# Sixteen-head attention sequence: GpSimd's work after making an input is put in another order

## The chip, the cores and the metric

One core of one Trainium2 chip runs the whole kernel in a single launch. The metric is the device time of one execution in microseconds (us), lower is better. The engines are TensorE (PE in the profile), VectorE (DVE), ScalarE (ACT), GpSimd (POOL) and the DMA queue of SyncE (SP). Each runs its own instructions in order and waits for the others through semaphores.

## The reference, cut to what matters

Two transformer-like layers over `x` of 32 entries x 128 tokens x 128 channels in float32, with a context of 32 x 120 x 128. Four stages: cross attention with 8 heads, a feed-forward network in which the 512 best of 1536 channels are chosen per entry group (`top_k`), cross attention with 16 heads over the context, and a last stage with latent self attention of 16 heads and a mixture of experts.

```python
x = x + _L0_xattn_ref(ctx_1024, _layernorm(x), mask, ...)
x = x + _L0_ffn_ref(_layernorm(x), Wm, Wp, Wc1, Wc2)   # top_k(ck, 512) after each of its steps
x = x + _L1_xattn_ref(_layernorm(x), ctx_1024, ctx_1024, mask, w_q, w_k, w_v, w_o)
x = x + _L1_ffn_ref(_layernorm(x), g1, Wq, Wdkv, Wuk, Wuv, Wo, g2, gate_w, w1, w2)
# _L1_ffn_ref: x = x + _mla(_rmsnorm(x, g1)); x = x + _moe(_rmsnorm(x, g2))
```

The change touches the two 16-head attentions alone, which one function (`attentions16`) runs as one sequence of 64 inputs.

## The kernel before

`mega_kernel` runs the stages one after the other: 8-head attention, feed-forward, the 16-head sequence, mixture of experts. In the 16-head sequence inputs 0 to 31 are the entries of the cross attention (120 keys, names with `l1`) and inputs 32 to 63 the same entries for the latent attention (128 keys, names with `mla`). `run_pair_steps` calls `body(n)` for n = -2 to 65 on each engine; even and odd steps are unrolled in some stretches and run in hardware loops (`Fori`) of two steps in the others. Nothing but the order of each `body` and the semaphores sets the order of the work: there is no planner.

What step n does, engine by engine, in the order of its queue:

- **TensorE**: turns (transposes) probability group 3 of input n-1, turns the normalised input n+1 (`turn_input`, L1482, waits for GpSimd's `z_made`), projects the output of n-2 (L1547), turns group 2 of n-1, projects q, k and v of n+1 (L1493 to L1495), multiplies groups 0 and 1 of n-1 with the values (L1536, L1539), turns group 1 of n, multiplies groups 2 and 3 of n-1, in even steps totals the search's counts (L1552), computes the scores of n+1 (L1509 bias, L1514, waits for `q_spread` and `k_copied`), turns group 0 of n.
- **VectorE**: copies the turned input n+1 out of PSUM (`copy_input`, L1453 or L1455), copies group 3 of n-1 (L1462), adds a projection (L1678), takes the second maximum (L1644), statistics (L1684), shifts scores (L1654), copies group 1 of n, copies the values of n+1 (L1470), inverts the sums (L1663), in even steps reads a digit of the search (`read_digit`, L1697), scales the output (L1669), and takes the first maximum of input n+1 (`max_a`, L1636). At the end of step 16 it has `second_half` of the search (L1703 to L1709 and the helper at L1261), at the end of steps 17 and 34 `mla_moments`.
- **ScalarE**: copies q (L1579), copies group 2 of n-1 (L1462), copies k (L1586), in even steps the third trial of a search round (`try_number`, L1610), the second exponential (`exp_b`, L1602), in odd steps the first two trials of the next round, copies group 0 of n (L1462), and the eight first exponentials of input n+1 (`exp_a`, L1594), which wait for `max_a`.
- **GpSimd**: makes the input n+1 (`centre` L1746, `norm_output` L1760 for the second layer only, `norm_input` L1754, which writes `zn`), spreads the queries of n+1 into `QX` (`spread_q`, L1767, waits for `q_copied`), then in even steps updates the search (`next_trials(k - 1)` with k = n // 2, four tiny operations L1777 to L1783, the first of which waits for the digit that VectorE reads in this step), and in some steps computes a power, that is inverse roots of variances (L125): `later_scales` in steps -2 to 1 and `mla_scales` in steps 18, 19, 34, 35, 36 and 37. The power of step 18 waits for the moments that VectorE takes at the end of step 17, the one of step 34 for those that it takes at the end of step 34.
- **SyncE** loads the contexts two inputs ahead.

The search finds the 512th largest of 1536 logits, two bits a round; its 16 rounds are spread over the first 34 steps, two steps each. A round is: three counts on ScalarE (two in an odd step, one in the even step after it), a total on TensorE, a digit on VectorE, an update of bounds on GpSimd. After eight rounds `second_half` makes the keys of the lower half.

Of the kernel before, what the change touches and what calls it, by code (L numbers as in the profile page):

```python
# [15 lines left out]
B = 32  # L16
# [1221 lines left out]
ROUNDS = 8  # L1238
# [28 lines left out]
CHANGE = 12  # L1267


def run_pair_steps(eng, body):  # L1270

    for n in range(-2, 4):
        body(n, n % 2, n // 2)
    with eng.Fori(0, ROUNDS - 2) as i:
        body(2 * i + 4, 0, i + 2, True)
        body(2 * i + 5, 1, i + 2, True)
    for n in range(2 * ROUNDS, 2 * ROUNDS + 4):
        body(n, n % 2, n // 2)  # L1280
    with eng.Fori(0, B // 2 - 3 - ROUNDS) as i:
        body(2 * i + 2 * ROUNDS + 4, 0, i + ROUNDS + 2, True)
        body(2 * i + 2 * ROUNDS + 5, 1, i + ROUNDS + 2, True)
    for n in range(B - 2, B + 6):
        body(n, n % 2, n // 2)
    with eng.Fori(0, B // 2 - 4) as i:
        body(2 * i + B + 6, 0, None, False)
        body(2 * i + B + 7, 1, None, False)
    for n in range(PAIR - 2, PAIR + 2):
        body(n, n % 2, None)  # L1290


def attentions16(nc, phase, psum, X2, X3, stats6, mean, rstd, mhalf, small, ident, ident_bf, cols,
# [8 lines left out]
    with ExitStack() as sems, ExitStack() as st:  # L1302
# [170 lines left out]
        with nc.Block() as block:  # L1473
# [157 lines left out]
            def _(dve):  # L1631
# [16 lines left out]
                def shift_b(n, par, l1):  # L1648
                    if there(n):
                        K = keys(n, l1)  # L1650
                        wait(dve, max_b_taken, n + 1)
                        wait(dve, turned[3], n - 1)
                        wait(dve, turned[2], n - 1)
                        dve.tensor_tensor(probs[par][:, 8:16, 0:K].rearrange("p (c j) k -> p c j k", c=2),  # L1654
                                          psum[:, 2:4, 0:4 * K].rearrange("p c (j k) -> p c j k", k=K),
                                          n_max[par][:, 8:16].rearrange("p (c j) -> p c j", c=2).unsqueeze(3).broadcast_to([P, 2, 4, K]),
                                          ALU.add).then_inc(b_shifted, 1)
# [54 lines left out]
                def body(n, par, k, l1=None):  # L1712
                    copy_input(dve, n + 1, l1)
                    copy_group(dve.tensor_copy, dve, n - 1, 3, l1)
                    add_projection(n - 2, l1)
                    max_b(n, par, l1)
                    take_stats(n - 2, l1)
                    shift_b(n, par, l1)
                    copy_group(dve.tensor_copy, dve, n, 1, l1)
                    copy_values(dve.tensor_copy, dve, n + 1, 1 - par, l1)  # L1720
                    if router and par == 0 and k is not None and round_there(k - 1):
                        wait(dve, totalled, k)
                    invert_sums(n - 1)
                    if router and par == 0 and k is not None:
                        read_digit(k - 1)
                    scale_out(n - 1)
                    max_a(n + 1, 1 - par, l1)
                    if router and par == 0 and isinstance(k, int) and k == ROUNDS:
                        second_half()
                    if isinstance(n, int) and n == 2 * ROUNDS + 1:  # L1730
                        mla_moments(slice(0, CHANGE), 6)
                    if isinstance(n, int) and n == B + 2:
                        mla_moments(slice(CHANGE, B), 12)
# [4 lines left out]
            @block.gpsimd  # L1738
            def _(pool):
                def centre(m, l1):  # L1740
                    if there(m):
                        l1 = is_l1(m, l1)
                        wait(pool, z_made, m)
                        if not l1:
                            wait(pool, x_out_made, m - B)
                        pool.tensor_tensor(centred[:, :], row(X2, m, l1), of_entry(mean if l1 else mla_mean, m, l1).broadcast_to([P, D]),  # L1746
                                           ALU.subtract).then_inc(x_centred, 1)

                def norm_input(m, l1):
                    if there(m):  # L1750
                        l1 = is_l1(m, l1)
                        wait(pool, x_centred, m + 1)
                        wait(pool, z_turned, m)
                        pool.tensor_tensor(zn[:, :], centred[:, :], of_entry(rstd if l1 else mla_scale, m, l1).broadcast_to([P, D]),  # L1754
                                           ALU.mult).then_inc(z_made, 1)

                def norm_output(m, l1):
                    if there(m) and not is_l1(m, l1):
                        wait(pool, x_centred, m + 1)
                        pool.tensor_tensor(row(X3, m, False), centred[:, :], of_entry(mla_rstd, m, False).broadcast_to([P, D]),  # L1760
                                           ALU.mult).then_inc(x_out_made, 1)

                def spread_q(m, par):
                    if there(m):
                        wait(pool, q_copied, m + 1)
                        wait(pool, scored, m - 1)
                        pool.tensor_tensor(QX[par][:, :, :], qT[:, :].unsqueeze(1).broadcast_to([P, 4, P]),  # L1767
                                           own_slots[:, :].unsqueeze(2).broadcast_to([P, 4, P]), ALU.mult).then_inc(q_spread, 1)

                def next_trials(k):  # L1770
                    if round_there(k):
                        t = search
                        wait(pool, digit_read, k + 1)
                        wait(pool, trials_ready, k)
                        if isinstance(k, int) and k == ROUNDS:
                            wait(pool, halved, 4)
                        pool.tensor_tensor(t["below"][:, :], t["below4"][:, :], t["digit4"][:, :], ALU.subtract).then_inc(below_made, 1)  # L1777
                        wait(pool, below_made, k + 1)
                        pool.tensor_tensor(t["bias"][:, :], t["offsets"][:, :], t["below"][:, :].broadcast_to([P, 3]), ALU.add).then_inc(bias_made, 1)
                        wait(pool, bias_made, k + 1)  # L1780
                        pool.tensor_tensor(t["below4"][:, :], t["below"][:, :], t["four"][:, :], ALU.mult).then_inc(below4_made, 1)
                        wait(pool, below4_made, k + 1)
                        pool.tensor_tensor(t["per_unit"][:, :], t["per_unit"][:, :], t["four"][:, :], ALU.mult).then_inc(trials_ready, 1)  # L1783

                def later_scales(n):
                    if isinstance(n, int) and n < 2:
                        inverse_roots(pool, rstd, small[:, 0, :], mhalf, slice(FIRST + 7 * (n + 2), FIRST + 7 * (n + 3))).then_inc(scales_made, 1)
                    if isinstance(n, int) and n == 2:
                        pool.wait_ge(scales_made, 4)

                def mla_scales(n):
                    half = CHANGE + (B - CHANGE) // 2
                    for at, some, ready in ((2 * ROUNDS + 2, slice(0, CHANGE), 3), (B + 2, slice(CHANGE, half), 5), (B + 4, slice(half, B), 5)):
                        if isinstance(n, int) and n == at:
                            pool.wait_ge(var_ready, ready)
                            inverse_roots(pool, mla_rstd, small[:, 0, :], mhalf, some).then_inc(mla_scales_made, 1)
                        if isinstance(n, int) and n == at + 1:
                            inverse_roots(pool, mla_scale, small[:, 1, :], mhalf, some).then_inc(mla_scales_made, 1)
                    if isinstance(n, int) and n in (B - 2, PAIR - 2):
                        pool.wait_ge(mla_scales_made, 2 if n < B else 6)  # L1800

                def body(n, par, k, l1=None):
                    centre(n + 1, l1)
                    norm_output(n + 1, l1)
                    norm_input(n + 1, l1)
                    spread_q(n + 1, 1 - par)
                    if router and par == 0 and k is not None:
                        next_trials(k - 1)
                    later_scales(n)
                    mla_scales(n)  # L1810

                run_pair_steps(pool, body)

            @block.sync
# [394 lines left out]
```

## Time and profile before

| | us |
|---|---|
| median of 3 runs | 1333.4 (1332.63 to 1336.6) |
| the profiled execution | 1335.86 |
| its span in the trace | 1333.7 |
| TensorE busy | 1230.1 (92%) |
| VectorE busy | 927.5 (70%) |
| ScalarE busy | 798.9 (60%) |
| GpSimd busy | 588.9 (44%) |

The 16-head sequence takes from about 598 to 1073 us of the span. A profile row gives an instruction (line of kernel.py, engine, operation), its start and duration, and in square brackets how long its engine sat idle before it and what released it. The times of a step are read here from one `max_a` (L1636) to the next, since each step has one.

### The profile page before, as it was taken

Reading aid. Unit: us, or ns where it says so; the run is one execution under the profiler, and the core shown is the slowest. Engines: PE = TensorE matmul, PEld = TensorE weight load, DVE = VectorE, ACT = ScalarE, POOL = GpSimd, SP = SyncE. Lnnn points to the kernel's source line nnn. Section 1 sums busy time; section 2 is a strip of 40 time slices with the busy share of each in tenths; the row PEclk is TensorE's granted clock in tenths of the full one; section 3 lists DMA queues with packets and bytes.
Section 4 is the critical chain, followed back from the end, with each engine's and each line's share of the span. In section 5 each row is a group of like instructions: output and inputs, shape, how many; then the busy total and the mean of one; then the engine's idle time right before and its main releaser. Section 6 shows DMA issues by size and latency. Waiting matters only on the chain. (4 is left out here: it accounts for less than half of the span.)

```text
span 1333.7 us, 37978 instructions
## 1 busy us (share of the span) xinstructions
PE 1230.1 (92%) x13719; PEld 879.3 (66%) x13719; DVE 927.5 (70%) x2003; ACT 798.9 (60%) x2101; POOL 588.9 (44%) x673
## 2 busy tenths in 40 slices
PE   1899999999999995978999899989999979999996
PEld 0466666666666663436777777768888847777775
DVE  6476676677677673766999889979999955343431
ACT  0578878878878862325777677756666633333332
POOL 3577566666656655104223332343333223333343
PEclk9899999999999997987999899989999979999998
DMA  8000000000000000000000002000000000000000
GB/s 216 13 1 1 0 0 0 0 0 0 0 0 0 0 1 1 0 4 10 11 9 8 10 10 69 3 2 1 0 0 0 0 1 9 9 8 8 8 11 16
DMA packets 22740, 14.71 MB, mean 11 GB/s; under 512 B 6378, under 2 KB 21610, under 8 KB 22540
## 3 DMA queue, kind: packets, MB, share of 16 engines
q1 hardware_dynamic: 22520, 13.75, 3.8%
q8 instruction: 43, 0.70, 0.2%
q14 instruction: 29, 0.24, 0.1%
q10 hardware_dynamic: 148, 0.01, 0.0%
HBM read 11.66 MB, written 2.10 MB: 10 GB/s over the span
## 5 line engine op out<-in xcount | busy, mean ns | idle before, releaser
L690 POOL TENSOR_TENSOR r_norm<-ssm,mhalf 128x24 f32<-128x24 f32 x32 | 134.9, 4215 | 162.7 <-DVE ssm L595 162.7
L1767 POOL TENSOR_TENSOR pair_QX<-pair_qT,own_slots 128x512 f32<-128x512 f32 x64 | 66.7, 1041 | 257.7 <-ACT pair_qT L1579 257.7
L1985 ACT ACTIVATE moe_hid<-psum 128x512 f32<-128x512 f32 x128 | 76.4, 598 | 137.5 <-PE psum L1919 137.5
L1525 PE MATMUL psum<-ident,pair_probs 128*120 128x128 f32 (+1 forms) x1024 | 154.6, 285 | 0.7 <-ACT pair_probs L1594 0.6
L533 ACT ACTIVATE l_probs<-psum,l_n_max 128x248 f32<-128x248 f32 x256 | 117.2, 481 | 57.7 <-DVE l_n_max L613 57.7
L2143 POOL TENSOR_TENSOR moe_acc<-moe_acc,moe_prod 128x512 f32<-128x512 f32 x64 | 81.3, 1271 | 147.4 <-DVE moe_prod L2099 147.4
L1594 ACT ACTIVATE pair_probs<-psum,pair_n_max 128x120 f32<-128x120 f32 (+1 forms) x512 | 137.7, 380 | 10.4 <-DVE pair_n_max L1636 5.0
L1929 PEld LDWEIGHTS psum<-w,moe_hid 128*128 128x128 f32 x1024 | 123.1, 192 | 26.8 <-issue 26.8
L2099 DVE TENSOR_TENSOR moe_prod<-psum,moe_combine 128x512 f32<-128x512 f32 x64 | 44.3, 692 | 135.8 <-PE psum L1929 135.7
L1525 PEld LDWEIGHTS psum<-ident,pair_probs 128*120 128x120 f32 (+1 forms) x1024 | 111.3, 141 | 28.6 <-issue 11.9
L1462 ACT COPY pair_probsT<-psum 120x512 f32<-120x512 f32 (+1 forms) x128 | 77.7, 607 | 86.4 <-PE psum L1525 86.2
L1929 PE MATMUL psum<-w,moe_hid 128*128 128x128 f32 x1024 | 123.4, 275 | 0.0
L1919 PE MATMUL psum<-moe_moe_hT,w 128*128 128x512 f32 x256 | 122.5, 606 | 0.0
L1536 PE MATMUL psum<-pair_probsT,V 120*32 120x128 f32 (+1 forms) x2048 | 107.2, 281 | 0.3 <-DVE X L1678 0.3
L1539 PE MATMUL psum<-pair_probsT,ONE 120*32 120x128 f32 (+1 forms) x2048 | 104.3, 275 | 0.0
L1462 DVE COPY pair_probsT<-psum 120x512 f32<-120x512 f32 (+1 forms) x128 | 87.2, 681 | 4.7 <-PE psum L1525 4.6
L697 POOL TENSOR_TENSOR qkn<-qk,r_norm 128x1536 f32<-128x1536 f32 x32 | 88.4, 2762 | 2.5
L1602 ACT ACTIVATE pair_probs<-pair_probs 128x960 f32<-128x960 f32 (+1 forms) x64 | 67.0, 1047 | 35.9 <-DVE pair_probs L1654 35.9
L1636 DVE TENSOR_REDUCE pair_n_max<-psum 128x8 f32<-128x960 f32 (+1 forms) x64 | 76.1, 1189 | 8.8 <-PE psum L1514 8.8
L640 DVE TENSOR_TENSOR outT<-psum,r_spread 128x256 f32<-128x256 f32 x64 | 26.9, 420 | 78.8 <-PE psum L441 73.3
L613 DVE TENSOR_REDUCE l_n_max<-psum 128x4 f32<-128x992 f32 x64 | 76.3, 1192 | 6.4 <-PE psum L397 2.4
L1514 PE MATMUL psum<-pair_kT,pair_QX 32*128 32x120 f32 (+1 forms) x2048 | 77.2, 287 | 0.0
(292 smaller groups left out, 2925.3 us busy)
## 6 DMA issues: line engine op xcount, KB each, us to landing
X<-x_in SPq DMA_DIRECT2D x8, 256.0 KB, 4.6
out_dram<-moe_acc SPq DMA_DIRECT2D x32, 64.0 KB, 1.5
CT<-ctx_in SPq DMA_DIRECT2D x8, 240.0 KB, 5.5
pair_cT<-ctxT_in SPq DMA_DIRECT2D x32, 60.0 KB, 1.8
w<-w_in SPq DMA_DIRECT2D x1, 1024.0 KB, 5.0
wm<-wm_in SPq DMA_DIRECT2D x1, 768.0 KB, 4.3
wp<-wp_in SPq DMA_DIRECT2D x1, 768.0 KB, 6.6
wkv<-wkv_in SPq DMA_DIRECT2D x1, 512.0 KB, 5.3
```

What stands on the lines that cost most here:

```text
L533: e = act.activation(probs[u][:, h, :], psum[:, 2 * u + h // 2, (h % 2) * K:(h % 2 + 1) * K], ACT.Exp, bias=n_max[u][:, h:h + 1], accum_ou ...
L690: pool.tensor_tensor(r_norm[:, :], ssm[:, :], mhalf[:, 0:3 * H], ALU.pow).then_inc(s["norm_inverted"], 1)
L697: pool.tensor_tensor(qkn[:, :, :].rearrange("p a (h d) -> p (a h) d", d=HD), qk[:, :, :].rearrange("p a (h d) -> p (a h) d", d=HD), r_norm ...
L1462: copy(probsT[0:K, g, :, :], psum[0:K, 4 + g % 2, :].rearrange("k (j q) -> k j q", j=4)).then_inc(copied[g], 1)
L1514: mm = pe.matmul(psum[:, t, s * K:(s + 1) * K], QX[par][32 * t:32 * t + 32, s, :], kT[par][32 * t:32 * t + 32, 0:K], start=False, stop=(s ...
L1525: tr = pe.transpose(psum[0:K, 4 + g % 2, j * P:(j + 1) * P], probs[par][:, 4 * g + j, 0:K], ident[:, :])
L1536: pe.matmul(psum[32 * tile:32 * tile + 32, 6, 0:P], V[par][0:K, g * P + 32 * tile:g * P + 32 * tile + 32], probsT[0:K, g, tile, :], start= ...
L1539: mm = pe.matmul(psum[32 * tile:32 * tile + 32, 6, P:2 * P], ONE[0:K, 32 * g:32 * g + 32], probsT[0:K, g, tile, :], start=False, stop=(g = ...
L1594: e = act.activation(probs[par][:, h, 0:K], psum[:, h // 4, (h % 4) * K:(h % 4 + 1) * K], ACT.Exp, bias=n_max[par][:, h:h + 1])
L1919: pe.matmul(psum[:, 2 + i % BANKS, :], w1[:, e, half * P:(half + 1) * P], hT[par][:, :], start=True, stop=True).then_inc(hidden[i], 1)
L1929: mm = pe.matmul(psum[:, 5 + e % 2, b * D:(b + 1) * D], hid[i % RING][:, b * P:(b + 1) * P], w2[:, i, :], start=(half == 0), stop=(half == ...
L2143: pool.tensor_tensor(a[:, :, :], a[:, :, :], prod[e % 2][:, :, :], ALU.add).then_inc(summed[e], 1)
```

## The change

Three places change. On GpSimd, the step now makes the input n+1, then does the search's update or a power if the step has one, and spreads the queries of n+1 last. The search's update moves from even steps to the odd step that follows, with the same k, and so stands behind the making of input n+2 and ahead of its spreading. The second and third pairs of powers move by two steps, from 34 to 37 to 36 to 39, and the moments of step 34 are then two steps old. On VectorE, `second_half` moves from the end of step 16 to the middle of step 17, behind `shift_b`, since it waits for the update that is now in step 17. `run_pair_steps` unrolls two more steps, 38 and 39, and its last loop starts two steps later, for all engines. No arithmetic, transfer or buffer changes.

```diff
@@ run_pair_steps
-    for n in range(B - 2, B + 6):
+    for n in range(B - 2, B + 8):
         body(n, n % 2, n // 2)
-    with eng.Fori(0, B // 2 - 4) as i:
-        body(2 * i + B + 6, 0, None, False)
-        body(2 * i + B + 7, 1, None, False)
+    with eng.Fori(0, B // 2 - 5) as i:
+        body(2 * i + B + 8, 0, None, False)
+        body(2 * i + B + 9, 1, None, False)
@@ vector: body
                     shift_b(n, par, l1)
+                    if router and par == 1 and isinstance(k, int) and k == ROUNDS:
+                        second_half()
                     copy_group(dve.tensor_copy, dve, n, 1, l1)
...
                     max_a(n + 1, 1 - par, l1)
-                    if router and par == 0 and isinstance(k, int) and k == ROUNDS:
-                        second_half()
@@ gpsimd: mla_scales
-                    for at, some, ready in ((2 * ROUNDS + 2, slice(0, CHANGE), 3), (B + 2, slice(CHANGE, half), 5), (B + 4, slice(half, B), 5)):
+                    for at, some, ready in ((2 * ROUNDS + 2, slice(0, CHANGE), 3), (B + 4, slice(CHANGE, half), 5), (B + 6, slice(half, B), 5)):
@@ gpsimd: body
                     norm_input(n + 1, l1)
-                    spread_q(n + 1, 1 - par)
-                    if router and par == 0 and k is not None:
+                    if router and par == 1 and k is not None:
                         next_trials(k - 1)
                     later_scales(n)
                     mla_scales(n)
+                    spread_q(n + 1, 1 - par)
```

## Rows read from the trace of the kernel before

**Rows 1.** Waits, longest first: waiter, what released it; us total, times, longest.

```profile
PE psum L1482 <- POOL pair_zn L1754: 23.7, 20, 5.1
DVE pair_zT L1453 <- PE psum L1482: 17.6, 15, 3.2
```

**Rows 2.** Timeline, step 13: start us, duration, instruction, [idle before, releaser].

```profile
701.70 0.19 POOL L1777 TENSOR_TENSOR below<-below,digit 128x1 f32<-128x1 f32 x1 [2.01 <-DVE totals L1697]
702.00 1.16 DVE L1636 TENSOR_REDUCE pair_n_max<-psum 128x8 f32<-128x960 f32 x1 [0.20 <-PE psum L1514]
702.51 0.19 POOL L1783 TENSOR_TENSOR per_unit<-per_unit,four 128x1 f32<-128x1 f32 x1
...
703.67 0.33 PE L1482 MATMUL psum<-ident,pair_zn 128*128 128x128 f32 x1 [0.72 <-POOL pair_zn L1754]
704.03 0.29 DVE L1453 COPY pair_zT<-psum 128x128 f32<-128x128 f32 x1 [0.88 <-PE psum L1482]
705.77 1.04 POOL L1767 TENSOR_TENSOR pair_QX<-pair_qT,own_slots 128x512 f32<-128x512 f32 x1 [2.15 <-ACT pair_qT L1579]
706.90 0.42 PE L1536 MATMUL psum<-pair_probsT,V 120*32 120x128 f32 x8
```

**Rows 3.** Timeline, the step after it (14, even, with a total of the search).

```profile
709.52 1.15 DVE L1636 TENSOR_REDUCE pair_n_max<-psum 128x8 f32<-128x960 f32 x1
713.15 1.04 POOL L1767 TENSOR_TENSOR pair_QX<-pair_qT,own_slots 128x512 f32<-128x512 f32 x1 [5.42 <-ACT pair_qT L1579]
713.59 0.16 PEld L1536 LDWEIGHTS psum<-pair_probsT,V 120*32 120x32 f32 x8 [0.17 <-ACT pair_probsT L1462]
716.51 1.16 DVE L1636 TENSOR_REDUCE pair_n_max<-psum 128x8 f32<-128x960 f32 x1 [0.20 <-PE psum L1514]
```

**Rows 4.** Timeline around the power of step 18.

```profile
742.95 1.04 POOL L1767 TENSOR_TENSOR pair_QX<-pair_qT,own_slots 128x512 f32<-128x512 f32 x1 [5.64 <-ACT pair_qT L1579]
745.80 1.17 PE L1514 MATMUL psum<-pair_kT,pair_QX 32*128 32x120 f32 x32
747.03 1.16 DVE L1636 TENSOR_REDUCE pair_n_max<-psum 128x8 f32<-128x960 f32 x1 [0.19 <-PE psum L1514]
747.60 2.27 POOL L125 TENSOR_TENSOR pair_mla_rstd<-small,mhalf 128x12 f32<-128x12 f32 x1
750.77 0.48 PE L1482 MATMUL psum<-ident,pair_zn 128*128 128x128 f32 x1 [2.79 <-POOL pair_zn L1754]
759.35 1.15 DVE L1636 TENSOR_REDUCE pair_n_max<-psum 128x8 f32<-128x960 f32 x1
```

**Rows 5.** Busy time by stretch: PE, PEld, DVE, ACT, POOL, granted clock, DMA.

```profile
753.00:757.00 4.00, 4.00 (x52) 2.93 (x55) 1.95 (x4) 3.16 (x8) 2.81 (x2) 0.52 0.09 19
```

**Rows 6.** Timeline around the powers of steps 34 to 37.

```profile
868.15 1.22 DVE L1636 TENSOR_REDUCE pair_n_max<-psum 128x8 f32<-128x1024 f32 x1
870.56 1.96 POOL L125 TENSOR_TENSOR pair_mla_rstd<-small,mhalf 128x10 f32<-128x10 f32 x1 [4.43 <-DVE small L1690]
882.29 1.22 DVE L1636 TENSOR_REDUCE pair_n_max<-psum 128x8 f32<-128x1024 f32 x1
889.04 1.23 DVE L1636 TENSOR_REDUCE pair_n_max<-psum 128x8 f32<-128x1024 f32 x1
903.30 1.23 DVE L1636 TENSOR_REDUCE pair_n_max<-psum 128x8 f32<-128x1024 f32 x1
```

**Rows 7.** Timeline, last search update's neighbourhood, first steps with 128 keys.

```profile
853.68 1.22 DVE L1636 TENSOR_REDUCE pair_n_max<-psum 128x8 f32<-128x1024 f32 x1 [0.21 <-PE psum L1514]
861.40 1.22 DVE L1636 TENSOR_REDUCE pair_n_max<-psum 128x8 f32<-128x1024 f32 x1
```

**Rows 8.** Timeline around the second half of the search, steps 16 and 17.

```profile
732.09 0.14 DVE L1703 TENSOR_SCALAR high<-below 128x1 f32<-128x1 f32 x1
733.77 0.28 DVE L1453 COPY pair_zT<-psum 128x128 f32<-128x128 f32 x1
```

**Rows 9.** The spreading's group, by tile: duration ns, min/median/max.

```profile
L1767 POOL TENSOR_TENSOR pair_QX<-pair_qT,own_slots x64: 1040/1041/1042, 603.6 to 1062.2; 128x512 f32<-128x512 f32 x64
```

## What the change was forecast to do

> **What bounds the kernel now.** I read the list of waits first, because the change reorders one engine's queue and adds no work. GpSimd is busy less than half of the span, yet TensorE waits for the input that it makes 20 times, 23.7 us in all, and VectorE in turn waits for the turned input, 17.6 us in the first layer alone [rows 1]. So the question is whether the input is late because GpSimd is late, or because it stands in its queue behind something that waits.
>
> The timeline of one pair of steps answers that. Step 13 starts with a first maximum at 702.00. GpSimd finished the spreading of the input before and then stood for 2.01 us until the digit came, updated the search from 701.70 to 702.70, and only then made the next input; TensorE had been idle 0.72 us when it turned it at 703.67, and VectorE 0.88 us when it copied it at 704.03 [rows 2]. The next step, whose predecessor has no update, has the input early: GpSimd idles 5.42 us before its spreading and no wait for the input stands in the rows [rows 3]. From maximum to maximum the first step takes 709.52 - 702.00 = 7.52 us and the second 716.51 - 709.52 = 6.99 [rows 2, 3]. Hence an operation of GpSimd off the path as to its own length holds the path by its place in the queue. The same shape in large: the powers. In step 18 a power of 2.27 us stands behind the update and ahead of the input, TensorE idles 2.79 us, and the step from 747.03 takes 12.32 us [rows 4]; the granted clock falls to 0.52 in 753 to 757 us, that is the lower level (1.2 GHz) after the idle time [rows 5]. After step 34 a power waits 4.43 us for VectorE's moments, and the step from 868.15 takes 14.14 us [rows 6].
>
> **The pieces and their prices.** *The update.* It goes from ahead of `centre` to behind `norm_input`. The inputs of steps with an update are then made right behind the spreading, as in the other steps, some two microseconds before TensorE wants them. What is late next? The step with the input in time shows a chain that does not touch GpSimd: first maximum, eight exponentials and the copies of q and of group 2 on ScalarE, third group's multiplication on TensorE. It runs from 709.52 to 713.59, 4.07 us, and the multiplication was released by ScalarE [rows 3]. From that multiplication to the next maximum the odd step takes 709.52 - 706.90 = 2.62 us [rows 2, 3]. The new odd step is thus 4.07 + 2.62 = 6.69 us instead of 7.52: 0.83 us each. It is an estimate joined from two halves. From above it is bounded by the 6.99 us of the even step, which carries a total on TensorE that the odd one lacks (gain 0.53), from below by VectorE's idle 0.88 plus the 0.1 or so that the pipeline of two of its operations hides (gain 1.0) [rows 2, 3]. I take 0.83, nearest to the rows of the same step. There are 16 updates; 12 of them stand in plain steps of 120 keys, the others are costed below. 12 x 0.83 = 10.0 us.
>
> Two steps of the second layer's head carry an update too; the one from 853.68 takes 7.72 us [rows 7], the other one much the same. A step of this layer without an update or a power takes 889.04 - 882.29 = 6.75 [rows 6]. 2 x 0.97 = 1.9 us.
>
> *The power of step 18.* It now stands ahead of the spreading of input 19, behind a wait for the moments of step 17. Input 20 is made before any of this matters, and the step from 747.03 falls from 12.32 to 6.69, with it the idle time and the low clock: 5.6 us [rows 2 to 5]. What hides the power: moments let a power start 870.56 - 868.15 = 2.41 us behind a maximum [rows 6], the spreading starts 713.15 - 709.52 = 3.63 behind it [rows 3]. A power of 2.27 then ends 4.68 behind it, and the spreading is 1.05 us late: it ends at 742.95 + 1.04 + 1.05 = 745.0 instead of 744.0. The scores multiply from 745.80, with some 0.4 us of bias by estimate ahead of them [rows 4], so 0.4 us of cover is left; beyond it, each microsecond would be one of that step. In step 19 update and second power follow each other: from 746.65 (a digit comes 0.3 us before the maximum, [rows 2]) 1.0 + 2.27 us end at 749.9. The spreading there may start 3.6 us behind the maximum, at 750.6 [rows 3]: covered with 0.7 us to spare.
>
> *The powers of steps 34 to 37.* They go to 36 to 39, where the moments of step 34 are long ready, and lie in the 4 to 5 us that GpSimd stands before its spreading [rows 3]; 1.96 us each [rows 6]. The moments on VectorE remain: the power started 870.56 - 868.15 = 2.41 us behind the maximum, of which 1.22 are the maximum, so they take about 1.2 us. The step falls from 14.14 to 6.75 + 1.2 = 7.95, that is 6.2 us. The two steps from 889.04 to 903.30 take 14.26 us instead of 13.50, since a power stands before the input there as well: 0.76, of which I keep back 0.15 for the entry of the loop, which falls two steps later and is not removed: 0.6 us [rows 6].
>
> *The second half.* It costs VectorE 733.77 - 732.09 = 1.68 us now and hides the late input of that step [rows 8]. In its new place it costs VectorE the same 1.68 us, and ScalarE's trial behind it starts some 0.8 us later, ahead of a copy that has to wait for VectorE's maximum anyway. I put the step at no change; between 0.1 us gained (the slack of VectorE) and 0.6 lost. Powers of steps -2 to 1, and the two unrolled steps: the first input stands behind its power in both orders, and the later ones were not waited for; 0, at most 0.3 us either way for the instructions of the longer program.
>
> Sum: 10.0 + 1.9 + 5.6 + 6.2 + 0.6 + 0 = 24.3 us. The profiled execution took 1335.86 us, 2.5 above the median of the runs; from it 1311.6, and from the median 1333.4 the forecast is **1309.1 us**. A check from the other side: of the 23.7 us that TensorE waits, 5.1 are the first input, which stays; 18.6 are to be had, to which the low clock behind the two long stalls adds [rows 1, 5].
>
> *GpSimd's work beside VectorE's.* The spreading lies beside maxima, shifts and copies of VectorE throughout, and takes 1040 to 1042 ns in all 64 cases [rows 9], so in this trace nothing of VectorE's mix held it up. The Trainium skill ("SBUF — State Buffer", section "SBUF: two separate sides") says that GpSimd and VectorE share a port pair under an exclusive lock, and that the loser blocks for the whole instruction. By that rule the powers, which now come to lie beside a working VectorE, could hold it up, and the time would be that of the second rival below. This trace agrees with the rule in nothing that it shows of GpSimd; whether VectorE is ever the one blocked no row here shows.
>
> **Rivals.**
> *The step stays at the length of its neighbour.* If what bounds the even step, 6.99 us, is not the search's total but the common chain, odd steps fall by 0.53 only: 12 x 0.53 + 2 x 0.7 = 7.8; the long stalls give 12.32 - 6.99 = 5.3 and 5.9; 0.3 for the rest. 19.3 us, 1314.1. For it: VectorE and TensorE are both near full in these steps. Against it: the step from 882.29 to 889.04 takes 6.75 with more keys [rows 6].
> *VectorE is blocked by the powers.* Each power that now lies beside a working VectorE would cost it the power's whole length: two of 2.27 and four of 1.96 us, 12.4 us [rows 4, 6]: 24.3 - 12.4 = 11.9, 1321.5. Against it stand the constant durations [rows 9].
> *Nothing moves.* The diff would not do what it says if the input were still late, for instance because `centre` waited for something that ends with the digit. It waits for `z_made` of its predecessor only, and in even steps GpSimd makes the input at once, which its idle time of 5.42 shows [rows 3]. 1333.4.
> *Slower: the spreading is held by the digit.* The scores need the spreading, and it now stands behind a wait for VectorE's digit in 16 steps. Today the digit's update is over at 702.70 and the spreading starts at 705.77 [rows 2]; made 0.3 us earlier by the shorter step, there are still some 2.8 us between. From the point at which the digit comes 2.8 us later than now, each microsecond is paid in all 16 steps; to lose the whole 24.3 it has to be 1.5 us beyond that, and at 2 us beyond it the kernel takes 24.3 - 32 = 8 us more, 1341. The digit stands ahead of the first maximum in VectorE's queue, so it can hardly come that late.
>
> **How the numbers follow.** Forecast 0.80; neighbour's length 0.12; blocked VectorE 0.03; nothing moves 0.02; slower 0.03. The bounds of the forecast's own terms: the update 0.53 to 1.0 us in 12 steps, that is 3.6 us less gain or 2.0 more; powers, second half and program about 2 us each way, by estimate; the median of a few runs another 2 (the runs before lie 4 us apart). Downwards 1309.1 - 2 - 2 - 2 = 1303; upwards the first rival's 1314.1 with some 3 of the same, 1317. Some 4 us (0.3%) are what a measurement of this kernel can tell from no change. Faster by more than that 0.95, within it 0.02, slower 0.03.
>
> **What the changed kernel would show.** In the list of waits TensorE's wait for the input has 1 or a few entries and about 5 us, the first input; GpSimd's wait for the digit shrinks from 2.0 us a time to 1 or less, as the input is made in it. From maximum to maximum: 6.7 in plain odd steps, 6.99 still in even ones, 6.7 for the step with the power of step 18, about 7.9 behind the moments of step 34, and a granted clock of 1.0 throughout. The spreading stays at an idle time of over 2 us before it in steps with an update. I am wrong if odd steps stay above 6.9, if TensorE begins to wait for the spread queries, or if a VectorE operation beside a power is longer than its like.

## The result and the profile after

The changed kernel takes 1314.23 us (median of 4 runs, 1312.16 to 1315.53), the kernel before 1334.32 beside it: ratio 0.985, interval 0.9838 to 0.9862, that is 1.4 to 1.6% faster. The forecast was 1309.1 with a range of 1303 to 1317. The profiled execution took 1314.13 us with a span of 1311.9, against 1335.86 and 1333.7.

The list of waits by tile answers [rows 1]: what the input `zn` waits for and who waits for it.

```profile
L1754 POOL TENSOR_TENSOR pair_zn<-pair_centred,rstd x32: 398/398/593, 601.2 to 817.4; 128x128 f32<-128x128 f32 x32
...
  PE psum L1482: 5.1, 1
  DVE pair_zT L1453: 4.1, 2
```

TensorE waits once, for the very first input, where it waited 20 times; the wait of 5.1 us that stays is the one the forecast set aside. GpSimd's wait for the digit, from the list of waits, is 18.6 / 16 = 1.2 us a time, where it was 32.8 / 16 = 2.05:

```profile
POOL pair_QX L1767 <- ACT pair_qT L1579: 234.4, 60, 4.8
POOL below L1777 <- DVE totals L1697: 18.6, 16, 2.6
```

The odd step that answers [rows 2], from its timeline (start, duration, instruction, idle before):

```profile
698.45 0.19 POOL L1777 TENSOR_TENSOR below<-below,digit 128x1 f32<-128x1 f32 x1 [1.10 <-DVE totals L1697]
698.76 1.16 DVE L1636 TENSOR_REDUCE pair_n_max<-psum 128x8 f32<-128x960 f32 x1 [0.20 <-PE psum L1514]
699.55 0.27 PE L1482 MATMUL psum<-ident,pair_zn 128*128 128x128 f32 x1
699.86 0.29 DVE L1453 COPY pair_zT<-psum 128x128 f32<-128x128 f32 x1
702.31 1.04 POOL L1767 TENSOR_TENSOR pair_QX<-pair_qT,own_slots 128x512 f32<-128x512 f32 x1 [2.86 <-ACT pair_qT L1579]
705.46 1.15 DVE L1636 TENSOR_REDUCE pair_n_max<-psum 128x8 f32<-128x960 f32 x1
```

Neither TensorE nor VectorE stands before the input, and the step takes 705.46 - 698.76 = 6.70 us instead of 7.52; the spreading keeps 2.86 us of room behind the update.

In the tables below a step runs from the first maximum (L1636) of its input to the next one, as in the forecast: step 13 is the one from 702.00 in [rows 2], step 19 the one of 12.32 us in [rows 4], step 35 the one of 14.14 us in [rows 6].

| us | before | changed |
|---|---|---|
| plain even step | 6.99 | 6.99 |
| plain odd step | 7.52 | 6.70 |
| step 17 (second half) | 8.19 | 8.38 |
| step 18 (moments) | 7.83 | 9.34 |
| step 19 | 12.32 | 6.71 |
| step 31, step 33 | 7.74, 7.72 | 6.72, 6.75 |
| step 35 (moments) | 14.14 | 7.87 |
| steps 37 to 39 | 21.01 | 20.56 |
| first maximum to the last of the sequence | 457.86 | 435.32 |

One row goes the wrong way: step 18. Its timeline in the changed kernel, and the stretches around it (columns: length of the stretch, busy time of PE, PEld, DVE, ACT and POOL, granted clock, busy share of the DMA engines, GB/s):

```profile
734.54 1.15 DVE L1636 TENSOR_REDUCE pair_n_max<-psum 128x8 f32<-128x960 f32 x1
734.68 0.49 PE L1547 MATMUL psum<-l_wo,pair_outT 128*128 128x128 f32 x2 [0.56 <-DVE pair_outT L1669]
...
735.61 0.17 DVE L857 TENSOR_TENSOR small<-stats 128x12 f32<-128x12 f32 x1
...
736.97 0.52 PE L1493 MATMUL psum<-pair_zT,l_wq 128*128 128x128 f32 x2 [1.36 <-DVE pair_zT L1453]
...
738.69 0.65 PE L1539 MATMUL psum<-pair_probsT,ONE 120*32 120x128 f32 x8
739.03 1.04 POOL L1767 TENSOR_TENSOR pair_QX<-pair_qT,own_slots 128x512 f32<-128x512 f32 x1
...
741.21 0.40 PE L1539 MATMUL psum<-pair_probsT,ONE 120*32 120x128 f32 x8
```

```profile
730.00:734.00 4.00, 3.98 (x92) 2.96 (x90) 3.93 (x13) 2.55 (x6) 1.70 (x3) 1.00 0.09 19
734.00:738.00 4.00, 2.08 (x14) 1.72 (x12) 3.86 (x15) 2.81 (x11) 1.20 (x1) 0.91 0.00 0
738.00:742.00 4.00, 4.00 (x71) 2.91 (x70) 2.72 (x4) 2.61 (x6) 2.83 (x4) 0.66 0.10 22
```

VectorE does the second half in the middle of step 17 (730.58 to 732.6) and the moments behind the maximum of 734.54 (from L857 at 735.61 to 736.7). The 3 us between them are full of other work, so it catches up with nothing: it is busy 3.93 and 3.86 of 4 us in the first two stretches. TensorE stands 0.56 and then 1.36 us for it, and its granted clock falls towards the lower level (1.2 GHz) for a part of the stretches: a group of eight multiplications takes 0.65 us at 738.69 and 0.40 at 741.21. The spreading, which the power of step 18 indeed holds up, ends at 740.07, two microseconds ahead of the scores; it is not what costs the time.

### The profile page after: what moved, and what is told of

The parts are those of the page before. It is cut to its first block and busy times, and to the rows that moved or that the text cites. A ratio compares the mean times of both kernels' runs of the same rounds, so it can differ in the third digit from the quotient of the medians.

```text
span 1311.9 us, 37944 instructions
## 1 busy us (share of the span) xinstructions
PE 1224.1 (93%) x13719; PEld 876.5 (67%) x13719; DVE 925.8 (71%) x2003; ACT 795.9 (61%) x2101; POOL 588.4 (45%) x673
## 3 DMA queue, kind: packets, MB, share of 16 engines
q1 hardware_dynamic: 22520, 13.75, 3.9%
## 5 line engine op out<-in xcount | busy, mean ns | idle before, releaser
L1636 DVE TENSOR_REDUCE pair_n_max<-psum 128x8 f32<-128x960 f32 (+1 forms) x64 | 76.0, 1188 | 8.8 <-PE psum L1514 8.8
```

## Experiments

Differences of a few tenths are read from the steps of the profiled executions; the medians carry some 1 us of scatter. Sequence stands for first to last first maximum.

**The second half put back.**

```diff
@@ vector: body
-                    if router and par == 1 and isinstance(k, int) and k == ROUNDS:
-                        second_half()
...
                     max_a(n + 1, 1 - par, l1)
+                    if router and par == 0 and isinstance(k, int) and k == ROUNDS:
+                        second_half()
```

> The changed kernel with the second half of the search put back to the end of step 16 on VectorE. In the changed kernel the step from the maximum at 734.54 takes 9.34 us where before it took 7.83; in it TensorE idles 1.36 + 0.56 us and the granted clock is 0.66 in 738 to 742 us. Theory (pile-up): second half in the middle of step 17 and moments at its end hold VectorE for 1.7 + 1.1 us within one step, TensorE runs dry and its clock falls to the lower level. Then here the two steps take about 8.3 and 7.8 us, the clock stays at 1.0, and the kernel is 1.5 us faster than the changed one, some 21.5 to 23 us faster than before. Rival (the power ahead of the spreading holds the scores of input 19): that step stays at 9.3. Second reading: the two big operations of the second half took 0.77 and 0.55 us in the changed kernel beside GpSimd's making of an input, 0.62 and 0.41 before. If GpSimd's work beside them is the cause, they take 0.6 and 0.4 here, where GpSimd stands idle.

1311.95 us, ratio to before 0.9834 (0.982 to 0.9847). Steps 17 and 18 take 8.19 and 7.83 us; the clock in the answering stretches:

```profile
734.00:738.00 4.00, 3.46 (x56) 2.60 (x58) 3.90 (x15) 3.75 (x14) 2.85 (x2) 1.00 0.09 22
738.00:742.00 4.00, 4.00 (x94) 3.29 (x86) 3.76 (x9) 1.68 (x3) 2.62 (x8) 1.00 0.00 0
```

The step is 1.5 us shorter with the clock at 1.0, as the theory has it. The rival falls: the power still stands ahead of the spreading of input 19, and the step is short. The second reading holds too. In the changed kernel, beside GpSimd's making of input 19:

```profile
730.76 0.77 DVE L1705 SCALAR_TENSOR_TENSOR low_here<-key,high,low 128x384 f32<-128x384 f32 x1
731.19 0.59 POOL L1754 TENSOR_TENSOR pair_zn<-pair_centred,rstd 128x128 f32<-128x128 f32 x1
731.45 0.55 DVE L1707 TENSOR_SCALAR above<-key,high 128x384 f32<-128x384 f32 x1
```

With the second half put back, where GpSimd stands idle beside it:

```profile
725.95 0.62 DVE L1705 SCALAR_TENSOR_TENSOR low_here<-key,high,low 128x384 f32<-128x384 f32 x1
726.49 0.41 DVE L1707 TENSOR_SCALAR above<-key,high 128x384 f32<-128x384 f32 x1
...
730.59 0.40 POOL L1754 TENSOR_TENSOR pair_zn<-pair_centred,rstd 128x128 f32<-128x128 f32 x1
```

**The update alone, the powers alone.** Both with the second half at the end of step 16.

```diff
@@ gpsimd: body, update alone
                         next_trials(k - 1)
+                    spread_q(n + 1, 1 - par)
                     later_scales(n)
                     mla_scales(n)
-                    spread_q(n + 1, 1 - par)
@@ mla_scales, update alone
-(B + 4, slice(CHANGE, half), 5), (B + 6, slice(half, B), 5)
+(B + 2, slice(CHANGE, half), 5), (B + 4, slice(half, B), 5)
@@ gpsimd: body, powers alone
-                    if router and par == 1 and k is not None:
-                        next_trials(k - 1)
                     later_scales(n)
                     mla_scales(n)
                     spread_q(n + 1, 1 - par)
+                    if router and par == 0 and k is not None:
+                        next_trials(k - 1)
```

> The update of the search moved as in the change, the powers left behind the spreading in steps 18, 19 and 34 to 37, second half at the end of step 16. Theory (place in GpSimd's queue): 12 plain odd steps fall from 7.52 to 6.70, two of the second layer from 7.7 to 6.75, and the step with the long stall of 12.32 falls to about 7, since the update no longer stands with the power ahead of the input; the stall of 14.14 us behind step 34 stays. Gain over the kernel before 9.8 + 2.0 + 5 = 17 us. Rival (the powers make most of the gain): under 10 us.

> The powers moved as in the change (ahead of the spreading, the later ones by two steps), the update left in even steps behind the spreading, second half at the end of step 16. Theory: plain odd steps stay at 7.52; the step of 12.32 becomes 7.5, the one of 14.14 becomes 7.9, the two with a late input behind it 6.75: 4.8 + 6.3 + 0.5 = 11.6 us faster than before. If the two parts did not overlap, the gains of this kernel and of the update alone would add up to the 22.5 us of the sequence; the theory says 17 + 11.6 = 28.6, since both remove the stall of step 18.

| us | before | update alone | powers alone | both (second half put back) |
|---|---|---|---|---|
| plain odd step | 7.52 | 6.71 | 7.52 | 6.70 |
| step 19 | 12.32 | 6.71 | 7.31 | 6.70 |
| step 35 | 14.14 | 13.75 | 7.87 | 7.86 |
| sequence | 457.86 | 439.75 | 445.63 | 433.70 |
| median (before 1334.84) | | 1318.22 | 1323.23 | 1311.95 |

The update alone is worth 18.1 us of the sequence, the powers alone 12.2, both 24.2. Of the overlap of some 6 us, 5.0 are step 19, which either part cures: 5.6 and 5.0, and 5.6 together. With the update alone a part of the stall only moves: step 20 takes 7.50 instead of 6.98. The rest of the overlap lies in steps 1, 3, 35 and 38, 0.3 to 0.4 us each. In step 19 of the kernel before it took both, update and power, to hold the input long enough; the forecast had put this step under the powers.

**The total multiplied twice.** What keeps even steps at 6.99?

```diff
@@ tensor: total_trials
+                        pe.matmul(psum[:, 6, 3 * P:3 * P + 12], router["same_entry"][:, :],
+                                  search["count"][:, :].unsqueeze(2).broadcast_to([P, 3, 4]), start=True, stop=True)
                         pe.matmul(psum[:, 6, 3 * P:3 * P + 12], router["same_entry"][:, :],
```

> The changed kernel with the total of the search multiplied twice in each even step (same result). It asks what keeps even steps at 6.99 us where odd ones now take 6.70. Theory (TensorE's total stands on the path): each of 16 even steps grows by the time of one more such multiplication, 0.2 us, so 3.2 to 3.5 us slower than the changed kernel. Rival (a common chain, the total has slack): no change.

1316.54 us. Even steps take 7.21 us, 0.22 more; odd ones 6.71. The total is on the path. The sequence as a whole is only 1.9 us longer than the changed kernel's, not 3.2 to 3.5. The main reason was not looked for: step 18 takes 8.05 here, 1.3 less than in the changed kernel, that is the 7.83 of before and the 0.22. TensorE has the same two waits, and this time the clock stays:

```profile
736.76 0.49 PE L1547 MATMUL psum<-l_wo,pair_outT 128*128 128x128 f32 x2 [0.56 <-DVE pair_outT L1671]
739.05 0.49 PE L1493 MATMUL psum<-pair_zT,l_wq 128*128 128x128 f32 x2 [1.36 <-DVE pair_zT L1453]
...
734.00:738.00 4.00, 3.10 (x47) 2.29 (x40) 3.93 (x15) 2.16 (x6) 0.00 (x0) 1.00 0.01 2
738.00:742.00 4.00, 2.95 (x60) 2.46 (x64) 3.90 (x12) 3.53 (x13) 3.12 (x2) 1.00 0.09 22
```

By this execution the whole 1.5 us of step 18 is the clock: with the same idle time and the clock at 1.0, the step costs what it did before. The idle time exposes the kernel to the fall and does not cost the time by itself. It is one execution, of a kernel with one multiplication more; whether chance or that multiplication kept the clock up is not shown.

**The moments a step earlier.**

```diff
-                    if isinstance(n, int) and n == 2 * ROUNDS + 1:
+                    if isinstance(n, int) and n == 2 * ROUNDS:
                         mla_moments(slice(0, CHANGE), 6)
```

> The changed kernel with the moments of step 17 taken at the end of step 16; the second half of the search stays in the middle of step 17. Both then lie in the time of one step, but with some 3 us of other work between them, where in the changed kernel they end on each other. Theory (TensorE runs dry twice close together and its clock falls): the two steps that take 8.38 + 9.34 us in the changed kernel take 16.0 to 16.3 here and the granted clock stays at 1.0. Rival (the VectorE work costs that much wherever it lies in these steps): 17.5 or more.

A single execution: 1313.43 us; steps 17 and 18 take 9.10 + 6.91 = 16.01 us, clock 1.0. The times are the expected ones, but the reason given is not the difference between the kernels: some 3 us of other VectorE work lie between second half and moments in the changed kernel too. What differs is TensorE's idle time. Its waits in step 18 are 0.56 and 0.34 us here, where they are 0.56 and 1.36 there. And after the run before this one it proves less than it seemed to: a clock that stays up may be chance.

**The room ahead of the spreading.**

```diff
                         next_trials(k - 1)
+                        for _ in range(2 if round_there(k - 1) else 0):
+                            pool.tensor_tensor(idle_work[:, _, :], rstd[:, 0:10], mhalf[:, 0:10], ALU.pow)
```

> The changed kernel with one idle power of 10 columns (some 1.96 us) on GpSimd behind each update of the search, ahead of the spreading, in the 16 odd steps. It measures the room there. In the changed kernel GpSimd stands 2.86 us before the spreading of these steps and the bias multiplications start 0.5 us behind its end. Theory (the room is 2.9 + 0.5 us): no step changes. Rival (the spreading is nearly on the path, as the forecast's slower case would have it): up to 2 us in each odd step. For the rule of the shared port: if a power blocked VectorE, its operations beside it would be longer and the odd steps too.

> The same with two idle powers, 3.92 us. Theory (room 2.9 + 0.5 us): the spreading starts 1.06 us late, its end is 0.55 us too late for the scores, so each of the 16 odd steps takes 7.25 instead of 6.70: 9 us slower than the changed kernel in all. Rival (a slack of 1 us more): no change.

One idle power: 1314.71 us, plain odd steps 6.70, even 6.99; only step 19, which has a real power as well, grows to 7.45. No operation of VectorE got longer to a degree that shows in a step. Two: 1324.73 us, plain odd steps 7.21 (expected 7.25), sequence 10.2 us longer than in the changed kernel (expected 9), of which 2.65 are step 19. Both times are those of single executions. There the spreading runs straight behind the powers and TensorE waits for it:

```profile
701.71 3.87 POOL L1810 TENSOR_TENSOR pair_idle_work<-rstd,mhalf 128x10 f32<-128x10 f32 x2
705.54 1.04 POOL L1768 TENSOR_TENSOR pair_QX<-pair_qT,own_slots 128x512 f32<-128x512 f32 x1
...
706.68 0.43 PE L1510 MATMUL psum<-l_bias,ident_bf 32*32 32x480 bf16 x16 [0.45 <-issue]
```

The room is thus 3.87 - 0.51 = 3.4 us, 2.86 + 0.5 as read. In step 17 of this run the spreading also lies beside the second half, whose first big operation takes twice its 0.62 us:

```profile
733.90 1.04 POOL L1768 TENSOR_TENSOR pair_QX<-pair_qT,own_slots 128x512 f32<-128x512 f32 x1
734.11 1.25 DVE L1706 SCALAR_TENSOR_TENSOR low_here<-key,high,low 128x384 f32<-128x384 f32 x1
```

**The total out of the path.** The run with two totals says that 0.3 us stands in each even step. This version (with moments at the end of step 16) totals a step later:

```diff
@@ tensor: body
                     project(n - 2, l1)
+                    if router and par == 1 and k is not None:
+                        total_trials(k - 1)
...
-                    if router and par == 0 and k is not None:
-                        total_trials(k - 1)
                     scores(n + 1, 1 - par, l1)
@@ vector: body
+                    if router and par == 1 and k is not None:
+                        read_digit(k - 1)
                     add_projection(n - 2, l1)
...
-                    if router and par == 0 and k is not None and round_there(k - 1):
-                        wait(dve, totalled, k)
                     invert_sums(n - 1)
-                    if router and par == 0 and k is not None:
-                        read_digit(k - 1)
```

> A version that the total multiplied twice points to: TensorE totals the search's counts in the odd step that follows, behind the projection, where it has some slack, instead of ahead of the scores of the even step; VectorE reads the digit behind its copy of group 3; moments at the end of step 16. Theory: the even steps fall from 6.99 to 6.7, as the total leaves the path, and odd ones stay at 6.70 or grow by 0.1, since TensorE has under 0.2 us of slack there and VectorE 0.3: 16 x 0.2 to 0.3 = 3 to 5 us faster than the changed kernel, apart from steps 17 and 18. Rival (the total only moves to another point of the same chain): odd steps grow by the 0.3 that even ones lose.

1310.11 us, ratio to before 0.9822 (0.9809 to 0.9836). Even and odd steps take 6.69 and 6.68: the total found real slack, and the rival falls. Step 19 takes 8.11, since the digit now comes later and update and second power run into the spreading. Both powers of 12 columns in step 18:

```diff
-                        if isinstance(n, int) and n == at + 1:
+                        if isinstance(n, int) and n == (at if at < B else at + 1):
```

> The version with the later total, with both powers of 12 columns in step 18 instead of one in 18 and one in 19. In the version before it the step of input 20 took 8.11 us: update and power on GpSimd together end late there, since the digit comes 2 us later than in the changed kernel. Theory: the step falls to 6.7; step 18, where GpSimd stands 4.8 us ahead of its spreading, holds 2 x 2.27 = 4.5 us at no cost beyond some tenths. 1.2 to 1.4 us faster than the version before it, 25 to 26 us faster than the kernel before. Rival: moments come too late in step 18 for two powers, and that step grows by what the other loses.

1307.60 us, ratio to before 0.9804 (0.9791 to 0.9817); step 19 takes 6.68, the sequence 428.74. It beats both kernels, the changed one by 6.2 us on the same chip. Its first power lies beside the second half. The power is 0.32 us longer for it, and VectorE's operations beside the running power are not (L1707 0.41 and L1709 0.56 us, as in the kernel before):

```profile
729.26 0.40 POOL L1752 TENSOR_TENSOR pair_zn<-pair_centred,rstd 128x128 f32<-128x128 f32 x1
729.37 0.70 DVE L1705 SCALAR_TENSOR_TENSOR low_here<-key,high,low 128x384 f32<-128x384 f32 x1
729.62 2.59 POOL L125 TENSOR_TENSOR pair_mla_rstd<-small,mhalf 128x12 f32<-128x12 f32 x1
730.00 0.41 DVE L1707 TENSOR_SCALAR above<-key,high 128x384 f32<-128x384 f32 x1
730.44 0.56 DVE L1709 TENSOR_TENSOR key<-low_here,above 128x384 f32<-128x384 f32 x1
732.17 2.26 POOL L125 TENSOR_TENSOR pair_mla_scale<-small,mhalf 128x12 f32<-128x12 f32 x1
```

**Both once more, side by side.**

> The changed kernel itself, run beside the next kernel and the version above on one chip, since the times so far come from different chips. Expected 1314 us with the kernel before at 1334, and if the low clock in the step behind the second half hangs on the moment at which the idle time falls (with the total multiplied twice the same two waits of 0.56 and 1.36 us passed at a clock of 1.0 and the step took 8.05), it may take 7.8 or 9.3 us here.

> The changed kernel with the second half at the end of step 16, beside the changed kernel. Expected 1.7 us less than it (0.2 for VectorE operations that GpSimd's reads lengthen, 1.5 for the clock), if the clock falls in most executions of the changed kernel; 0.2 to 0.5 less if it fell in the profiled one only.

The changed kernel 1313.84 us (0.9836 to 0.9867 of before), the one with the second half put back 1313.52 (0.9838 to 0.9868). Their profiled steps repeat: 8.40 + 9.35 us and 8.20 + 7.83, sequences of 435.17 and 433.80. The medians do not show the 1.4 us; 0.3 lies within the scatter of the runs. That the second half put back is faster is shown for the profiled executions, not for the kernel's time.

## Why the prediction was right, point by point

*The update: right, in mechanism and size.* Forecast 12 x 0.83 = 10.0; the twelve steps give 9.8, 0.80 to 0.82 each but for 0.89 in the first. The two halves of the chain, 4.07 and 2.62, join to 6.69, and 6.70 came. Steps 31 and 33 gave 2.0 for 1.9. The rival with 6.99 in all steps falls, since even steps owe their 0.3 to the total. That the place in the queue is the cause is shown by the update alone, which moves nothing else in these steps and gives 6.71.

*Step 19: right in size, loosely attributed.* 5.6 forecast under the powers, 5.61 measured, but the update alone gives as much in this step, and pays 0.5 of it back in the next. The forecast's room of 0.7 us in that step stands as 0.71 us of idle time before the spreading. (Its sum starts at 746.65, where its rows give 747.03 - 0.30 = 746.73, which changes nothing.)

*Step 35 and the later powers.* 6.2 and 0.6 forecast; 6.27 and 0.45 measured. The entry of the loop cost 0.32 in step 39 instead of the 0.15 kept back; in the second profile of the same kernel that step takes 6.78 instead of 7.07, so it comes and goes.

*The second half: the step that failed.* The forecast put the pair of steps at "no change; between 0.1 us gained and 0.6 lost". They lost 1.7: 0.19 in step 17, where two VectorE operations are 0.15 and 0.14 longer beside GpSimd's making of an input, and 1.51 in step 18. The forecast had looked at the second half and at the moments one by one, each against its own neighbours, and not at both within 6 us on a VectorE without idle time, with TensorE dry behind them and its clock at stake. Of what it said the changed kernel would show, the granted clock of 1.0 throughout failed here. It had used the clock's fall to explain the old stalls and not asked where the change makes a new one.

*Sum.* Forecast 24.3, sequence 22.5; of the missing 1.8, 1.7 are this pair of steps. The span fell by 21.8, since the stages ahead of the sequence took 0.9 more in this execution. The medians fell by 20.1 on one chip and 19.2 on the other. So the larger part of what the forecast of 24.3 missed in the medians, 2.4 of 4.2 us, lies between the medians and the sequence, and it is not traced: the profiled execution of before was one of its slower ones (1335.86 with a median of 1333.4), and only one execution of each was profiled there.

*The port.* VectorE blocked by the powers, at 12.4 us, did not come. Beside the power of step 19 five VectorE operations keep their durations. All five read PSUM; but two that read SBUF alone keep theirs as well, beside the running power of the version with both powers together (0.41 and 0.56 us). What came is smaller and elsewhere. The Trainium skill ("SBUF — State Buffer", section "SBUF: two separate sides") names a VectorE operation with two inputs from SBUF against a GpSimd one that reads SBUF as a case in which one waits for the whole of the other. For GpSimd's multiplications the traces agree. The first big operation of the second half has two such inputs; it ends 0.41 to 0.42 us behind the GpSimd operation beside which it began: 731.53 behind 731.11 in the changed kernel (0.77 us long), 735.36 behind 734.94 with two idle powers (1.25 us), 730.07 behind 729.66 with both powers together (0.70 us). So its stretch is what was left of the other, not a fixed share. For the power they do not: it held neither of the two operations behind it, and was itself 0.32 us longer (2.59).

*Slower: the digit holds the spreading.* Measured room 3.4 us, forecast 2.8 and some. It did not come near, though GpSimd's wait for the digit is 1.2 us a time and not 1 or less. TensorE waits for the spread queries once in the sequence, 1.5 us, as before.

## What to carry to other kernels

An engine that is under half busy can still set the pace by the order of its queue: put what the bottleneck needs next ahead of whatever waits, and look at each wait for what stands behind it. Two parts that cure the same stall don't add up; run each alone before crediting one. When work is moved onto a full engine, look at what else lies in the same step there, and count a possible clock fall wherever the move lets TensorE run dry.

## What the runs showed of the hardware

- The granted clock fell in all four profiled executions in which TensorE waited 0.56 and then 1.36 or 1.37 us in step 18: the changed kernel (0.66 in four microseconds, step of 9.34), the same again (9.35), and with one and two idle powers (9.34 and 9.20). In a fifth, with the total multiplied twice, the same two waits left it at 1.00 (step of 8.05, 0.22 of it the second total). One wait of 1.19 us (second half put back) left it at 1.00 too.
- Operations of VectorE and GpSimd that read SBUF held each other up: 0.62 to 0.77 and to 1.25 us, and 0.41 to 0.55 us on VectorE, 0.40 to 0.59 and 2.27 to 2.59 on GpSimd. A GpSimd power that was already running did not hold up VectorE operations of 0.41 and 0.56 us.
- A multiplication of 12 columns costs a full 0.22 us where TensorE is on the path, and nothing that can be read behind the projection, where it has slack (odd steps of 6.68 us).
